# Second attention scores in two 32x64 tiles per key half, without late keys against early queries, odd heads reversed

## The chip, the cores and the metric

The program runs on one core of one Trainium2 chip. The metric is the time of one execution on the device in microseconds (us), as the median of several runs; lower is better.

## The reference

One decoder layer: a causal self attention with a latent side branch, a cross attention to a second input, and a slot mixer. The input has 64 sequences of 128 tokens of 256 values; both attentions have 16 heads of 16 values. What matters here is this, in both attentions, for every sequence and head:

```
scores = (q . k) / 4                    # 128 queries x 128 keys
scores = where(allowed, scores, NEG)    # self attention: key < query; cross attention: key <= query
attn   = softmax(scores, over keys)
out    = attn . v
```

So of each 128 x 128 square the quarter in which the keys are among the last 64 and the queries among the first 64 never counts.

## The kernel before

Everything is float32 but for the masks and the maxima (bfloat16). Three stages run one after the other, local_attention, cross_attention and slots, each over 32 pairs of sequences in a software pipeline. In each stage every engine has its own hand-written order (the functions `step`), and semaphores join them. In the cross attention the chain for the pair in work is, on TensorE (PE): first scores of sequence 0, first scores of sequence 1, second scores of sequence 0, second scores of sequence 1, values of sequence 0 and (one turn later) of sequence 1, with projections and transposes of the following pair between them.

The scores are computed twice.

- **First scores** (`scores`, L518 and L524 in the local stage, L1322 and L1328 in the cross stage): queries on the partitions. 16 small bfloat16 matmuls put the mask in (L1322), and 16 float32 matmuls with tiles of 32 rows and 64 columns add the products (L1328), 128 or 256 columns moving each. VectorE (DVE) takes the row maxima (L861, L1595) and splits each into two bfloat16 parts in `max_part`; PE turns them with one transpose through `ident_bf` (L538, L1340), and ScalarE (ACT) copies them to `max_t` (`copy_max`).
- **Second scores** (`scores_t`, L548 and L554, L1350 and L1356): keys on the partitions, as the product with the values wants them. Heads lie four to a bank, slot j of bank i; the bank index i is also the group of 32 rows of the array. 16 float32 matmuls (L1350) have a weight tile of 32 rows x 128 keys and 128 query columns moving. Then 16 bfloat16 matmuls (L1356), also of 32 rows x 128 columns, subtract the maxima through `slot_rows`. The last one lets ACT take the exponential of all four banks in one instruction (`exp`, L709, L1522).

GpSimd (POOL) zeroes what the mask forbids with four selects of four heads each (`mask_weights`, L1060, L1736); `values` (L570, L1372) waits for one select per four heads. A float32 matmul is four instructions in the trace: load, matmul, load, matmul (two passes). Each stage has 64 calls of `scores_t`.

The projections of keys (`project_k`) and values (`project_v`, L442 and L1283) are float32 matmuls with all 128 rows and columns of the array, with 256 (or 272) columns moving. In the step of ACT, `copy_max` of the previous pair stands ahead of `evac_k` of the present one.

Of the kernel before, what the change touches and what calls it, by code (L numbers as in the profile page):

```python
# [6 lines left out]
BF16 = mybir.dt.bfloat16  # L7
ALU = mybir.AluOpType
# [75 lines left out]
def decoder(nc, a, out):  # L84
    with ExitStack() as ctx:
# [12 lines left out]
        ident_bf = sb("ident_bf", [128, 128], BF16)  # L98
        with ExitStack() as kept:
            cross = CrossWeights(nc, kept, sem)  # L100
            with ExitStack() as scope:
                local_attention(nc, scope, sem, a, score_banks, side_banks, x_sb, ident, ident_bf, cross)
            slot_weights = SlotWeights(nc, kept, sem, a)
            with ExitStack() as scope:
                cross_attention(nc, scope, sem, a, score_banks, bank, x_sb, ident, ident_bf, cross, slot_weights)
            with ExitStack() as scope:
                slots(nc, scope, sem, a, out, bank, x_sb, ident, cross, slot_weights)
# [59 lines left out]
class CrossWeights:  # L167


    def __init__(self, nc, scope, sem):  # L170
# [19 lines left out]
        self.v_heads = [sb(f"v_heads{i}", [128, 2, H, HW]) for i in range(2)]  # L190
        self.max_part = sb("max_part", [128, 2, 128], BF16)
# [12 lines left out]
def local_attention(nc, scope, sem, a, score_banks, side_banks, x_sb, ident, ident_bf, cross):  # L204
# [45 lines left out]
    xn_t = sb("xn_t", [128, C, PT])  # L250
    pooled = sb("pooled", [128, C, 128])
# [49 lines left out]
    xnT_filled, xnT_ready, pooled_ready = s("xnT_filled"), s("xnT_ready"), s("pooled_ready")  # L301
    q_filled, q_ready, k_filled, k_ready = s("q_filled"), s("q_ready"), s("k_filled"), s("k_ready")
# [26 lines left out]
    with nc.Block() as block:  # L329
# [55 lines left out]
        def _(pe):  # L385
# [9 lines left out]
            def project(dst, e, first):  # L395
                for c in range(C):
                    mm = pe.matmul(dst[:, e * PT:e * PT + PT], w_qk[:, c, first + e, :], xn_t[:, c, :],  # L397
                                   start=(c == 0), stop=(c == C - 1), skip_group_check=True)
                return mm
# [33 lines left out]
            def project_v(at, tt):  # L433
                if tt == 0:
                    pe.wait_ge(k_ready, at.count(1, 1))
# [5 lines left out]
                for c in range(C):  # L441
                    mm = pe.matmul(v_bank[tt][:, 0:VW], xn_t[:, c, S * tt:S * tt + S], w_v[:, c, 0:VW],  # L442
                                   start=(c == 0), stop=(c == C - 1), skip_group_check=True)
# [53 lines left out]
            def slot(i, j):  # L497
                return score_banks[:, i, 128 * j:128 * j + 128]

            def scores(at, tt):  # L500
                if tt == 0:
                    pe.wait_ge(q_ready, at.count(1, 1))
                    pe.wait_ge(k_ready, at.count(1, 1))
                    if at.off == 0:
                        pe.wait_ge(masks_made, 14)
                        pe.wait_ge(zeroed, 13)
# [14 lines left out]
                for late in range(2):  # L521
                    for e in range(2):
                        for i in range(4):
                            mm = pe.matmul(near_far(half(e), i)[:, :, 128 * (1 - late):128 * (1 - late) + 64 * (1 + late)],  # L524
                                           q_f[at.par][group(i), e, S * tt + 64 * late:S * tt + 64 * late + 64],
                                           k_z[at.par][group(i), e, :, S * tt:S * tt + 64 * (1 + late)],
# [3 lines left out]
            def max_transpose(at, tt):  # L530
# [28 lines left out]
            def values(at, tt):  # L559
# [5 lines left out]
                for h in range(H):  # L565
                    g, j = h // 4, h % 4
                    slot_j = 2 * (j % 2) + j // 2
                    if j == 0:
                        pe.wait_ge(masked, at.count(8, 4 * tt + g + 1))
                    mm = pe.matmul(av_bank[HW * j:HW * j + HW, 128 * g:128 * g + 128], v_heads[at.par][:, tt, h, :],  # L570
                                   probs_t[tt][:, 4 * g + slot_j, :], start=True, stop=True, skip_group_check=True)
# [73 lines left out]
            pe.wait_ge(ident_made, 2)  # L645
# [4 lines left out]
        def _(act):  # L650
            def copy_xn(at):
# [3 lines left out]
                                     ACT.Copy).then_inc(xnT_ready, 1)  # L655

# [43 lines left out]
            def copy_max(at, tt):  # L700
                act.wait_ge(maxT_filled, at.count(2, tt + 1))
                wait(act, sct_filled, at.count(2, tt - 1))
                nc.scalar.activation(max_t[:, tt, :], maxT_bank[:].bitcast(BF16)[:, 0:128],
# [32 lines left out]
            def step(at):  # L736
# [8 lines left out]
                if at.real:  # L745
                    evac_k(at)
# [32 lines left out]
        def _(dve):  # L779
# [241 lines left out]
            dve.wait_ge(zeroed, 6)  # L1021
            nc.vector.memset(lat_rows[0:2, :], 0.0).then_inc(zeroed, 1)
# [6 lines left out]
            dve.wait_ge(zeroed, 13)  # L1029
# [15 lines left out]
        def _(pool):  # L1045
# [9 lines left out]
            def mask_weights(at, tt):  # L1055
                pool.wait_ge(exp_done, at.count(2, tt + 1))
                pool.sem_inc(pool_turn, 1)
                for g in range(4):
                    probs = probs_t[tt][:, 4 * g:4 * g + 4, :]
                    nc.gpsimd.affine_select(out=probs, in_=probs, pattern=[[0, 4], [1, 128]], compare_op=ALU.is_ge,  # L1060
                                            fill=0.0, base=-1, channel_multiplier=-1).then_inc(masked, 1)
# [57 lines left out]
            pool.wait_ge(ident_made, 1)  # L1119
            nc.gpsimd.tensor_copy(ident_bf[:], ident[:]).then_inc(ident_made, 1)  # L1120
# [32 lines left out]
def cross_attention(nc, scope, sem, a, score_banks, bank, x_sb, ident, ident_bf, cross, slot_weights):  # L1153
# [24 lines left out]
    ctx_t = sb("ctx_t", [128, C, PT])  # L1178
    q_f = [sb(f"q_f{i}", [128, 2, PT]) for i in range(2)]
# [22 lines left out]
    xnT_filled, xnT_ready, ctxT_filled, ctxT_ready = s("xnT_filled"), s("xnT_ready"), s("ctxT_filled"), s("ctxT_ready")  # L1202
    q_filled, q_ready, k_filled, k_ready = s("q_filled"), s("q_ready"), s("k_filled"), s("k_ready")
# [20 lines left out]
    with nc.Block() as block:  # L1224
# [17 lines left out]
        def _(pe):  # L1242
# [18 lines left out]
            def project(dst, e, first, src):  # L1261
                for c in range(C):
                    mm = pe.matmul(dst[:, e * PT:e * PT + PT], cross.w_qk[:, c, first + e, :], src[:, c, :],  # L1263
                                   start=(c == 0), stop=(c == C - 1), skip_group_check=True)
# [12 lines left out]
            def project_v(at, tt):  # L1277
                if tt == 0:
                    pe.wait_ge(k_ready, at.count(1, 1))
                else:  # L1280
                    pe.wait_ge(q_ready, at.count(1, 1))
                for c in range(C):
                    mm = pe.matmul(v_bank[tt][:, 0:D], ctx_t[:, c, S * tt:S * tt + S], cross.w_v[:, c, :],  # L1283
                                   start=(c == 0), stop=(c == C - 1), skip_group_check=True)
# [19 lines left out]

            def slot(i, j):
                return score_banks[:, i, 128 * j:128 * j + 128]

            def scores(at, tt):
# [16 lines left out]
                for late in range(2):  # L1325
                    for e in range(2):
                        for i in range(4):
                            mm = pe.matmul(near_far(half(e), i)[:, :, 128 * (1 - late):128 * (1 - late) + 64 * (1 + late)],  # L1328
                                           q_f[at.par][group(i), e, S * tt + 64 * late:S * tt + 64 * late + 64],
                                           k_z[at.par][group(i), e, :, S * tt:S * tt + 64 * (1 + late)],  # L1330
# [3 lines left out]
            def max_transpose(at, tt):  # L1334
# [5 lines left out]
                pe.transpose(maxT_bank[:].bitcast(BF16)[:, 0:128], max_part[:, tt, :], ident_bf[:]).then_inc(maxT_filled, 1)  # L1340

            def scores_t(at, tt):
# [4 lines left out]
                toks = slice(S * tt, S * tt + S)  # L1347
                for j in range(4):
                    for i in range(4):
# [905 lines left out]
```

## Time and profile before

| | us |
|---|---|
| median of three runs | 1481.04 (1479.7 to 1481.35) |
| the profiled execution | 1480.41 |
| its span in the profile | 1478.7 |
| PE busy | 1407.6 (95%) |
| DVE busy | 1088.6 (74%) |
| ACT busy | 900.5 (61%) |
| POOL busy | 823.5 (56%) |
| mean granted TensorE clock | 0.982 of full speed |

The span is counted from the first to the last instruction; 1.7 us lie around it. Engines: PE is TensorE's matmuls, PEld its weight loads, which overlap them. A busy PE is not PE at its peak, since matmuls are pipelined and overlap; what a block of them costs is read from where the next block starts. By the timeline the local stage ends near 690 us and the cross stage near 1165 us. L12 is line 12 of the kernel.

### The profile page before, as it was taken

How to read it: one execution, taken by the hardware profiler on the slowest of the kernel's cores; microseconds unless marked ns; L12 is line 12 of the kernel's file. 1: busy time of each engine (PE TensorE's matmuls, PEld its weight loads, DVE VectorE, ACT ScalarE, POOL GpSimd, SP SyncE). 2: the span in 40 equal slices, each digit the busy share in tenths (PEclk: the TensorE clock that was granted, in tenths of full speed). 3: DMA queues.
4: the chain of work that ended last, by engine and by line, in shares of the span. 5: the costliest groups of instructions: out<-in, count | busy, mean ns of one | idle time of the engine just before them, and what ended most of it. 6: DMA issues, size and time to landing. Idle time of an engine off the chain costs nothing. (4 is left out here: it accounts for less than half of the span.)

```text
span 1478.7 us, 57208 instructions
## 1 busy us (share of the span) xinstructions
PE 1407.6 (95%) x22238; PEld 1064.8 (72%) x22238; DVE 1088.6 (74%) x3025; ACT 900.5 (61%) x1573; POOL 823.5 (56%) x1152
## 2 busy tenths in 40 slices
PE   6999999999999999996999999999999949999997
PEld 4777777777777777774777777777777726766675
DVE  6777777777777777763477777777777748999996
ACT  2555555555555655553667676666667537778774
POOL 3455445554455544554377777877777753333442
PEclk9999999999999999997999999999999969999999
DMA  5500000000000000000300000000000000101111
GB/s 164 156 4 1 0 0 0 0 0 0 0 0 0 0 0 0 1 2 18 109 17 16 20 14 21 14 21 14 21 14 14 3 1 16 37 29 35 35 36 43
DMA packets 31207, 32.40 MB, mean 22 GB/s; under 512 B 3937, under 2 KB 29602, under 8 KB 31138
## 3 DMA queue, kind: packets, MB, share of 16 engines
q1 hardware_dynamic: 31138, 31.46, 6.9%
q8 instruction: 46, 0.75, 0.2%
q14 instruction: 23, 0.19, 0.0%
HBM read 23.06 MB, written 8.39 MB: 21 GB/s over the span
## 5 line engine op out<-in xcount | busy, mean ns | idle before, releaser
L1060 POOL TENSOR_SCALAR_AFFINE_SELECT a_probs_t<-a_probs_t 128x512 f32<-128x512 f32 x256 | 162.4, 669 | 62.2 <-ACT a_probs_t L709 62.2
L1595 DVE TENSOR_REDUCE c_neg_max<-score_banks 128x8 f32<-128x512 f32 (+1 forms) x128 | 116.6, 953 | 82.7 <-PE score_banks L1328 82.7
L1074 POOL TENSOR_TENSOR a_less<-a_attn,a_remote 128x512 f32<-128x512 f32 x32 | 40.8, 1274 | 218.1 <-DVE a_attn L884 218.1
L1736 POOL TENSOR_SCALAR_AFFINE_SELECT c_probs_t<-c_probs_t 128x512 f32<-128x512 f32 x256 | 153.8, 638 | 14.6 <-ACT c_probs_t L1522 13.8
L709 ACT ACTIVATE a_probs_t<-score_banks 128x2048 f32<-128x2048 f32 x64 | 120.2, 1878 | 47.0 <-PE score_banks L554 47.0
L1522 ACT ACTIVATE c_probs_t<-score_banks 128x2048 f32<-128x2048 f32 x64 | 120.3, 1879 | 26.2 <-PE score_banks L1356 26.2
L397 PE MATMUL side_banks<-a_xn_t,a_w_qk 128*128 128x256 f32 x512 | 134.7, 398 | 1.6 <-ACT a_xn_t L654 0.7
L861 DVE TENSOR_REDUCE a_neg_max<-score_banks 128x8 f32<-128x512 f32 (+1 forms) x128 | 116.4, 951 | 5.9 <-PE score_banks L524 5.9
L397 PEld LDWEIGHTS side_banks<-a_xn_t,a_w_qk 128*128 128x128 f32 x512 | 93.2, 197 | 13.0 <-issue 2.3
L2164 POOL TENSOR_TENSOR r_hn<-rz_t,half_hn 128x256 f32<-128x256 f32 x32 | 23.3, 729 | 138.5 <-ACT rz_t L1992 138.5
L664 ACT ACTIVATE a_k_z<-side_banks,a_b_k,row_half 128x256 f32<-128x256 f32 x128 | 61.8, 563 | 53.7 <-PE side_banks L397 53.7
L1529 ACT ACTIVATE c_av_t<-side_banks 128x512 f32<-128x512 f32 x64 | 39.2, 612 | 86.9 <-PE side_banks L1372 86.9
L1927 PE MATMUL side_banks<-w_ih,gi_t 128*128 128x512 f32 (+1 forms) x256 | 88.0, 486 | 0.4 <-DVE n_in L2093 0.3
L1485 ACT ACTIVATE c_k_z<-side_banks,b_k_half,row_half 128x256 f32<-128x256 f32 x128 | 61.9, 563 | 34.2 <-PE side_banks L1263 34.2
L1747 POOL TENSOR_TENSOR c_scaled<-c_normed,gamma 128x512 f32<-128x512 f32 x32 | 40.6, 1268 | 73.0 <-DVE c_normed L1577 73.0
L1350 PEld LDWEIGHTS score_banks<-c_q_f,c_k_z 32*128 32x128 f32 x2048 | 62.9, 186 | 22.6 <-ACT c_probs_t L1522 12.1
L548 PE MATMUL score_banks<-a_q_f,a_k_z 32*128 32x128 f32 x2048 | 75.1, 283 | 2.7 <-DVE a_neg_max L861 2.7
L548 PEld LDWEIGHTS score_banks<-a_q_f,a_k_z 32*128 32x128 f32 x2048 | 62.9, 186 | 19.7 <-DVE a_neg_max L861 13.0
L1350 PE MATMUL score_banks<-c_q_f,c_k_z 32*128 32x128 f32 x2048 | 75.1, 283 | 1.8 <-ACT c_probs_t L1522 1.8
L442 PE MATMUL side_banks<-a_w_v,a_xn_t 128*128 128x272 f32 x256 | 74.2, 412 | 0.0
L1927 PEld LDWEIGHTS side_banks<-w_ih,gi_t 128*128 128x128 f32 x256 | 48.4, 190 | 35.2 <-issue 31.5
L826 DVE TENSOR_TENSOR v_heads<-side_banks,a_b_v 128x272 f32<-128x272 f32 x64 | 28.0, 437 | 57.7 <-issue 49.3
(264 smaller groups left out, 3901.9 us busy)
## 6 DMA issues: line engine op xcount, KB each, us to landing
x_sb<-in_x SPq DMA_DIRECT2D x32, 256.0 KB, 3.0
ctx_in<-in_ctx SPq DMA_DIRECT2D x32, 256.0 KB, 2.7
out<-y SPq DMA_DIRECT2D x32, 256.0 KB, 2.1
w_ih<-in_ffn_w_ih SPq DMA_DIRECT2D x1, 768.0 KB, 4.8
w_hh<-in_ffn_w_hh SPq DMA_DIRECT2D x1, 768.0 KB, 6.0
a_raw_qk<-in_attn_qk_w SPq DMA_DIRECT2D x1, 512.0 KB, 3.8
a_raw_cross<-in_xattn_qk_w SPq DMA_DIRECT2D x1, 512.0 KB, 4.6
b_ih<-in_ffn_b_ih SPq DMA_DIRECT2D x1, 384.0 KB, 6.6
```

Source lines behind the costliest of these rows:

```text
L397: mm = pe.matmul(dst[:, e * PT:e * PT + PT], w_qk[:, c, first + e, :], xn_t[:, c, :], start=(c == 0), stop=(c == C - 1), skip_group_check= ...
L442: mm = pe.matmul(v_bank[tt][:, 0:VW], xn_t[:, c, S * tt:S * tt + S], w_v[:, c, 0:VW], start=(c == 0), stop=(c == C - 1), skip_group_check= ...
L548: pe.matmul(slot(i, j), k_z[at.par][group(i), j // 2, j % 2, toks], q_f[at.par][group(i), j // 2, toks], start=(j == 0), stop=False, skip_ ...
L709: nc.scalar.activation(probs_t[tt][:].rearrange("p h q -> p (h q)"), score_banks[:].rearrange("p b n -> p (b n)"), ACT.Exp, scale=SCALE).t ...
L861: ins = nc.vector.tensor_reduce(neg_max[:, tt, :].rearrange("p (i s l) -> p i s l", i=4, s=2)[:, :, :, late], all_scores[:, :, :, 128 * (1 ...
L1060: nc.gpsimd.affine_select(out=probs, in_=probs, pattern=[[0, 4], [1, 128]], compare_op=ALU.is_ge, fill=0.0, base=-1, channel_multiplier=-1 ...
L1350: pe.matmul(slot(i, j), k_z[at.par][group(i), j // 2, j % 2, toks], q_f[at.par][group(i), j // 2, toks], start=(j == 0), stop=False, skip_ ...
L1485: ins = nc.scalar.activation(k_z[at.par][:, e, half, :], k_bank[:, e * PT:e * PT + PT], ACT.Relu, bias=cross.b_k[:, half, e:e + 1], scale= ...
L1522: nc.scalar.activation(probs_t[tt][:].rearrange("p h q -> p (h q)"), score_banks[:].rearrange("p b n -> p (b n)"), ACT.Exp, scale=SCALE).t ...
L1595: ins = nc.vector.tensor_reduce(neg_max[:, tt, :].rearrange("p (i s l) -> p i s l", i=4, s=2)[:, :, :, late], all_scores[:, :, :, 128 * (1 ...
L1736: nc.gpsimd.affine_select(out=heads, in_=heads, pattern=[[0, 4], [1, 128]], compare_op=ALU.is_ge, fill=0.0, base=0, channel_multiplier=-1) ...
L1927: mm = pe.matmul(gate_bank[b][:, 0:hi - lo], gi_t[:, c, :], w.w_ih[:, c, lo:hi], start=(c == 0), stop=(c == C - 1))
```

## The change

In both attentions (not only in the cross attention) the second scores leave out the quarter of late keys and early queries. Each of the 16 matmuls of `scores_t` becomes two with weight tiles of 32 rows x 64 keys: the early keys with all 128 queries, the late keys with the 64 late queries. For odd heads (e = 1) keys and queries are taken in reverse order, so that the short product of an odd head falls into the half of the array that has the long product of the even head. The order of the heads in the banks changes to j = 2s + e. The left-out quarter is filled by the 16 maxima matmuls, which remain 32 x 128: two more rows of `max_part` are set to -1e30, and `slot_rows` has a one there for the keys concerned.

What the reversal brings with it: the key projection of odd heads reads its moving operand backwards; ACT makes a reversed copy of the transposed input (`reverse`, once per pair, between `copy_max` and `evac_k`); `project_v` takes 4 matmuls with half the columns in place of 2; the first scores, the second scores and the values read one moving operand backwards for odd heads; the transpose of the maxima becomes a bfloat16 matmul with the matrix `turned`; the selects go over every second head, and `values` waits for two selects per eight heads. Six small DVE instructions are added ahead of the first loop, one small POOL cast is removed.

The core of the diff (the cross attention; the local one has the same edits, with xn_rev for ctx_rev):

```diff
             def project(dst, e, first, src):
                 for c in range(C):
-                    mm = pe.matmul(dst[:, e * PT:e * PT + PT], cross.w_qk[:, c, first + e, :], src[:, c, :],
-                                   start=(c == 0), stop=(c == C - 1), skip_group_check=True)
+                    toks = src[:, c, :].rearrange("p (t k) -> p t k", t=2)
+                    mm = pe.matmul(dst[:, e * PT:e * PT + PT], cross.w_qk[:, c, first + e, :],
+                                   toks[:, :, ::-1] if first and e else toks, start=(c == 0), stop=(c == C - 1), skip_group_check=True)
...
             def project_v(at, tt):
                 if tt == 0:
+                    pe.wait_ge(reversed_, at.count(1, 1))
                     pe.wait_ge(k_ready, at.count(1, 1))
...
-                for c in range(C):
-                    mm = pe.matmul(v_bank[tt][:, 0:D], ctx_t[:, c, S * tt:S * tt + S], cross.w_v[:, c, :],
-                                   start=(c == 0), stop=(c == C - 1), skip_group_check=True)
+                for e in range(2):
+                    for c in range(C):
+                        toks = (ctx_rev if e else ctx_t)[:, c, S * tt:S * tt + S]
+                        mm = pe.matmul(v_bank[tt][:, 0:D].rearrange("p (h e n) -> p e h n", e=2, n=HD)[:, e],
+                                       toks,
+                                       cross.w_v[:, c, :].rearrange("p (h e n) -> p e h n", e=2, n=HD)[:, e],
+                                       start=(c == 0), stop=(c == C - 1), skip_group_check=True)
...
-                pe.transpose(maxT_bank[:].bitcast(BF16)[:, 0:128], max_part[:, tt, :], ident_bf[:]).then_inc(maxT_filled, 1)
+                pe.matmul(maxT_bank[:, 0:128], max_part[:, tt, :], cross.turned[:], start=True, stop=True,
+                          skip_group_check=True).then_inc(maxT_filled, 1)
...
-                toks = slice(S * tt, S * tt + S)
                 for j in range(4):
-                    for i in range(4):
-                        pe.matmul(slot(i, j), k_z[at.par][group(i), j // 2, j % 2, toks],
-                                  q_f[at.par][group(i), j // 2, toks], start=(j == 0), stop=False, skip_group_check=True)
+                    e = j % 2
+                    for late in range(2):
+                        rows, early, side = half(late ^ e), S * tt + 64 * late, late * (1 - e)
+                        for i in range(4):
+                            keys = k_z[at.par][group(i), e, j // 2, S * tt:S * tt + S][:, 64 * (late ^ e):64 * (late ^ e) + 64]
+                            queries = q_f[at.par][group(i), e, early:S * tt + S]
+                            pe.matmul(score_banks[rows, i, 128 * j + 64 * side:128 * j + 64 * side + 64 * (2 - late)],
+                                      keys, queries[:, ::-1] if e else queries,
+                                      start=(j == 0), stop=False, skip_group_check=True)
...
-                        by_row = score_banks[:, i, :].rearrange("p (e j r) -> p j e r", e=2, j=4)
-                        mm = pe.matmul(by_row[:, j], cross.slot_rows[group(i), j, :],
+                        quarters = score_banks[:, i, :].rearrange("p (s b r) -> p s b r", s=2, r=64)[:, j // 2]
+                        mm = pe.matmul(quarters[:, 1:3, :] if j % 2 else quarters[:, 0::3, :], cross.slot_rows[group(i), j, :],
...
-                    if j == 0:
-                        pe.wait_ge(masked, at.count(8, 4 * tt + g + 1))
+                    if h % 8 == 0:
+                        pe.wait_ge(masked, at.count(8, 4 * tt + g + 2))
...
+            def reverse(at):
+                act.wait_ge(ctxT_ready, at.count(1, 1))
+                wait(act, v_filled, at.count(2, 0))
+                nc.scalar.activation(ctx_rev[:].rearrange("p c (t k) -> p (c t) k", t=2),
+                                     ctx_t[:].rearrange("p c (t k) -> p (c t) k", t=2)[:, :, ::-1],
+                                     ACT.Copy).then_inc(reversed_, 1)
```

## Rows read from the trace of the kernel before

**Rows 1.** Page, part 1: busy time of each engine, its share, instructions.

```profile
PE 1407.6 (95%) x22238; PEld 1064.8 (72%) x22238; DVE 1088.6 (74%) x3025; ACT 900.5 (61%) x1573; POOL 823.5 (56%) x1152
```

**Rows 2.** Busy time by stretch (us, PE, PEld, DVE, ACT, POOL, clock, DMA, GB/s).

```profile
300.00:400.00 100.00, 99.26 (x1756) 75.64 (x1757) 72.86 (x182) 57.01 (x98) 54.02 (x70) 1.00 0.00 0
900.00:1000.00 100.00, 98.92 (x2014) 77.97 (x2007) 74.73 (x186) 65.90 (x111) 76.07 (x108) 1.00 0.07 18
```

**Rows 3.** Page, part 5: the score matmuls of both stages, with their counts.

```profile
L548 PE MATMUL score_banks<-a_q_f,a_k_z 32*128 32x128 f32 x2048 | 75.1, 283 | 2.7 <-DVE a_neg_max L861 2.7
L1350 PE MATMUL score_banks<-c_q_f,c_k_z 32*128 32x128 f32 x2048 | 75.1, 283 | 1.8 <-ACT c_probs_t L1522 1.8
```

**Rows 4.** Timeline, PE, cross stage, from 803 us (start us, busy us, engine, line).

```profile
803.12 1.03 PE L1263 MATMUL side_banks<-c_ctx_t,w_qk_b 128*128 128x256 f32 x4
803.99 1.03 PE L1263 MATMUL side_banks<-c_xn_t,w_qk_b 128*128 128x256 f32 x4
...
804.95 1.17 PE L1350 MATMUL score_banks<-c_q_f,c_k_z 32*128 32x128 f32 x32
...
805.94 0.40 PE L1356 MATMUL score_banks<-c_max_t,slot_rows 32*128 32x128 bf16 x16
...
806.27 1.13 PE L1263 MATMUL side_banks<-c_xn_t,w_qk_b 128*128 128x256 f32 x4
...
808.32 1.17 PE L1350 MATMUL score_banks<-c_q_f,c_k_z 32*128 32x128 f32 x32
...
810.61 0.60 PE L1292 MATMUL side_banks<-ident,c_q_f 128*128 128x128 f32 x4
...
811.05 0.60 PE L1257 MATMUL side_banks<-ident,ctx_in 128*128 128x128 f32 x4
```

**Rows 5.** Timeline, PE, local stage: the latent projections with 64 columns of the array.

```profile
301.22 0.66 PE L421 MATMUL side_banks<-a_xn_t,a_w_lat 128*64 128x128 f32 x8
...
301.70 0.40 PE L426 MATMUL side_banks<-a_pooled,a_w_lat 128*64 128x64 f32 x8
...
302.04 0.66 PE L429 MATMUL side_banks<-a_w_v,a_pooled 128*128 128x64 f32 x4
```

**Rows 6.** Timeline, PE: start of one call of the first scores.

```profile
816.68 0.32 PE L1322 MATMUL score_banks<-mask_b,mask_to_b 32*64 32x128 bf16 x16
```

**Rows 7.** That call: L1328 loads started by 816.86, 816.95, 817.00 and 817.15 us.

```profile
L1328 PEld LDWEIGHTS score_banks<-c_k_z,c_q_f x16: 128/132/133, 816.8 to 816.8; 32*64 32x64 f32 x16
L1328 PEld LDWEIGHTS score_banks<-c_k_z,c_q_f x17: 128/132/133, 816.8 to 816.9; 32*64 32x64 f32 x17
L1328 PEld LDWEIGHTS score_banks<-c_k_z,c_q_f x20: 127/132/133, 816.8 to 817.0; 32*64 32x64 f32 x20
L1328 PEld LDWEIGHTS score_banks<-c_k_z,c_q_f x32: 127/132/133, 816.8 to 817.1; 32*64 32x64 f32 x32
```

**Rows 8.** One line's instructions in one call: duration ns min/median/max, first and last start.

```profile
L1322 PE MATMUL score_banks<-mask_b,mask_to_b x16: 214/226/238, 816.7 to 816.8; 32*64 32x128 bf16 x16
L1350 PE MATMUL score_banks<-c_q_f,c_k_z x32: 270/270/372, 804.9 to 805.9; 32*128 32x128 f32 x32
```

**Rows 9.** Timeline, cross stage: ACT's work between PE blocks, and PE behind it.

```profile
804.19 1.93 ACT L1485 ACTIVATE c_k_z<-side_banks,b_k_half,row_half 128x256 f32<-128x256 f32 x4 [1.04 <-PE side_banks L1263]
...
806.38 1.88 ACT L1522 ACTIVATE c_probs_t<-score_banks 128x2048 f32<-128x2048 f32 x1 [0.26 <-PE score_banks L1356]
...
813.53 0.63 ACT L1529 ACTIVATE c_av_t<-side_banks 128x512 f32<-128x512 f32 x1
...
814.22 0.66 PE L1383 MATMUL side_banks<-ident,c_av_t 128*128 128x128 f32 x4
```

**Rows 10.** Timeline, cross stage: the selects of sequence 1 and the values that use them.

```profile
813.34 2.40 POOL L1736 TENSOR_SCALAR_AFFINE_SELECT c_probs_t<-c_probs_t 128x512 f32<-128x512 f32 x4
...
815.67 1.08 PE L1372 MATMUL side_banks<-c_probs_t,v_heads 128*32 128x128 f32 x32
```

**Rows 11.** Timeline: DVE's first wait for PE after its set-up.

```profile
17.63 0.35 DVE L814 TENSOR_SCALAR a_rq_f<-side_banks,a_b_lat 128x128 f32<-128x128 f32 x1 [2.70 <-PE side_banks L429]
```

More of the change, by code:

```diff
@@ L745, in step @@
                 if at.real:
+                    reverse(at)
                     evac_k(at)
@@ L1021, in _ @@
             dve.wait_ge(zeroed, 6)
+            for e in range(2):
+                turned = ident[:, 64 * e:64 * e + 64]
+                nc.vector.tensor_copy(cross.turned[:, 64 * e:64 * e + 64], turned[:, ::-1] if e else turned).then_inc(zeroed, 1)
+                early = cross.slot_rows[:, 0::2, 64 * (1 - e):64 * (1 - e) + 64]
+                nc.vector.tensor_scalar(early, early, cross.diagonal[:, 8 + e:9 + e], None, ALU.add).then_inc(zeroed, 1)
+                nc.vector.memset(max_part[64 * e:64 * e + 64, :, 8 + e::32], NEG).then_inc(zeroed, 1)
             nc.vector.memset(lat_rows[0:2, :], 0.0).then_inc(zeroed, 1)
@@ L1057, in mask_weights @@
                 pool.sem_inc(pool_turn, 1)
[L1058 to L1061, printed above, removed]
+                for g in range(2):
+                    for e in range(2):
+                        four, sign = probs_t[tt][:, 8 * g + e:8 * g + 8:2, :], 1 - 2 * e
+                        nc.gpsimd.affine_select(out=four, in_=four, pattern=[[0, 4], [sign, 128]], compare_op=ALU.is_ge,
+                                                fill=0.0, base=-1, channel_multiplier=-sign).then_inc(masked, 1)
             def bias_x(at):
@@ L1262, in project @@
                 for c in range(C):
-                    mm = pe.matmul(dst[:, e * PT:e * PT + PT], cross.w_qk[:, c, first + e, :], src[:, c, :],
-                                   start=(c == 0), stop=(c == C - 1), skip_group_check=True)
+                    toks = src[:, c, :].rearrange("p (t k) -> p t k", t=2)
+                    mm = pe.matmul(dst[:, e * PT:e * PT + PT], cross.w_qk[:, c, first + e, :],
+                                   toks[:, :, ::-1] if first and e else toks, start=(c == 0), stop=(c == C - 1), skip_group_check=True)
                 return mm
@@ L1278, in project_v @@
                 if tt == 0:
+                    pe.wait_ge(reversed_, at.count(1, 1))
                     pe.wait_ge(k_ready, at.count(1, 1))
@@ L1339, in max_transpose @@
                     pe.wait_ge(maxT_ready, at.count(2, 1))
-                pe.transpose(maxT_bank[:].bitcast(BF16)[:, 0:128], max_part[:, tt, :], ident_bf[:]).then_inc(maxT_filled, 1)
+                pe.matmul(maxT_bank[:, 0:128], max_part[:, tt, :], cross.turned[:], start=True, stop=True,
+                          skip_group_check=True).then_inc(maxT_filled, 1)
             def scores_t(at, tt):
@@ L1346, in scores_t @@
                     pe.wait_ge(exp_done, at.count(2, 1))
-                toks = slice(S * tt, S * tt + S)
                 for j in range(4):
-                    for i in range(4):
-                        pe.matmul(slot(i, j), k_z[at.par][group(i), j // 2, j % 2, toks],
-                                  q_f[at.par][group(i), j // 2, toks], start=(j == 0), stop=False, skip_group_check=True)
+                    e = j % 2
+                    for late in range(2):
+                        rows, early, side = half(late ^ e), S * tt + 64 * late, late * (1 - e)
+                        for i in range(4):
+                            keys = k_z[at.par][group(i), e, j // 2, S * tt:S * tt + S][:, 64 * (late ^ e):64 * (late ^ e) + 64]
+                            queries = q_f[at.par][group(i), e, early:S * tt + S]
+                            pe.matmul(score_banks[rows, i, 128 * j + 64 * side:128 * j + 64 * side + 64 * (2 - late)],
+                                      keys, queries[:, ::-1] if e else queries,
+                                      start=(j == 0), stop=False, skip_group_check=True)
                 pe.wait_ge(maxT_ready, at.count(2, tt + 1))
```

81 lines of the change are left out of this document (47 added, 34 removed).

## Prediction

> **What bounds the kernel now.** I read the page first: PE is busy 95% of the span, the next engine 74% [rows 1]. Then the busy time by stretch: in the steady part of both attention stages PE is busy for 99 of 100 us at full clock, and nobody else over 78 (the weight loads) [rows 2]. Then PE's timeline. So in both stages the time is PE's order of work, block after block, and an edit is worth what it adds to or takes from the distance between the starts of two blocks. Two prices hide between the blocks. Four passes of 256 columns take 0.87 us (803.12 to 803.99), but 0.96 us when a block with another tile shape follows (803.99 to 804.95): PE stands 0.09 us at a change of tile shape [rows 4]. And the score block of 32 instructions, 8 rounds of four tiles side by side, takes 0.99 us (804.95 to 805.94), where 8 rounds at 0.110 us (four passes of 128 columns in the 0.44 us from 810.61 to 811.05) make 0.88: the first pass after a change costs about 0.11 more [rows 4]. With loads of 64 columns that extra is smaller: 301.22 to 301.70 is 0.48 us for four rounds of 0.110, so 0.04 to 0.05 [rows 5]. A call of the second scores with the maxima takes 804.95 to 806.27 = 1.32 us, of which 0.33 us belong to the 16 maxima and the change of shape behind them. There are 2 x 2048 / 32 = 128 calls [rows 3].
>
> **The change, part by part.**
>
> (1) *The columns saved.* A half of the array gets 128, 64, 128 and 64 columns in place of four times 128, two passes each. A 64-column round is 0.06 us: 301.70 to 302.04 is 0.34 us for four rounds and a change of 0.09 [rows 5]. If both halves are always fed, the block is 2 x (0.11 + 0.06 + 0.11 + 0.06) + 0.05 = 0.73 us. That is 0.26 us less than 0.99, and 33 us over 128 calls; this is what the edit is good for at best.
>
> (2) *The instructions it takes.* The block goes from 64 instructions (loads and matmuls) to 128, all of them short. What happens beyond 64 is visible in the first scores. Their first matmul starts at 816.68 [rows 6]. 16 mask matmuls with their loads are 32 instructions, the 16 loads of L1328 started by 816.86 stand for another 32; in the next 0.09 us just one load starts, and then three in 0.05 us, 0.017 us apart, each the head of a float32 matmul of four instructions; all 32 have started by 817.15 [rows 7]. So 64 instructions stand ready, and the 65th and later come in only when the first of them are through: the first mask matmul lasts 0.214 us [rows 8], and the stream resumes some 0.05 us after that. I read it as a queue of 64 whose places come free in order. In the new block the first 64 instructions are j = 0 and j = 1. They run to 0.05 + 2 x (0.11 + 0.06) = 0.39 us. The first matmul's second pass starts at 0.16 us, lasts 0.27 us [rows 8] and is through at 0.43. The loads of j = 2 then come at 0.48, 0.50, 0.51 and 0.53 (128 columns) and up to 0.60 (64 columns), those of j = 3 from 0.61 to 0.66 and up to 0.73. With 0.05 us per load, the half that runs the short products of j = 2 is free at 0.72 to 0.77, and the long ones of j = 3 follow on it for 0.22 us: the block ends at 0.94 to 0.99. I take 0.97 us; bounds are 0.91 (places free 0.06 earlier) and 1.05 (later by as much again).
>
> (3) *A change of shape within the call.* The 32x64 block is followed by maxima in 32x128. No row shows just this pair of shapes. The bounds are nothing, since the rows of the array are cut in the same way, and 0.09 us, which every change in the rows costs, also the one from 128x64 to 128x128, where only the columns change [rows 4, 5]. I take 0.09, as that row is the nearest. The Trainium skill (TensorEngine Tiling (Array Packing), Key Properties) says that a change of tiling mode, not of the tile alone, drains the engine; the rows agree with 0.09 us each, and by it this change is paid too. The first round of the maxima also pays an extra of 0 to 0.05 us; I take 0.03.
>
> (4) *Sum per call.* 0.97 + 0.09 + 0.03 + 0.33 = 1.42 us against 1.32: 0.10 us more, 128 times, +12.8 us. It breaks even with a block of 0.87 us.
>
> (5) *project_v.* Four passes of 0.217 become eight of 0.110: +0.01 us. In the cross stage both calls lie in stretches that end on ACT anyway: the exponential ends at 806.38 + 1.88 = 808.26 and PE's next score block starts at 808.32; the copy ends at 814.16 and PE starts at 814.22 [rows 4, 9]. There it is free; without that cover it would be 0.6 us in all. In the local stage it counts: 64 x 0.01 = +0.6 us.
>
> (6) *ACT's reversed copy.* 512 elements like the copy of 0.63 us, in a place where ACT waits 1.04 us for the key projection [rows 9]. Nothing; were the gap gone, 0.6 us per pair, 20 us per stage. PE's new wait for it comes several blocks later, with the second sequence's projections queued behind it.
>
> (7) *Selects and waits.* The last eight heads wait for the fourth select, which ends at 815.74; PE reaches them at 815.67 + 0.54 = 816.21 [rows 10]. Covered by 0.47 us, nothing; the first eight have over 1 us. The selects are as large as before.
>
> (8) *Set-up.* Six small DVE instructions, well under 2 us together, ahead of a wait of 2.70 us for PE [rows 11]. Nothing. The turning of the maxima stays one bfloat16 matmul with 128 columns.
>
> (9) *Backward reads.* No row shows one. Bound below: nothing, as it is the same number of elements. Above: a pass of double length. I take nothing: every change named above leaves the count of elements alone, and the upper end is rival D.
>
> The profiled execution of 1480.4 us becomes 1480.4 + 12.8 + 0.6 = 1493.8; the median of the runs lies 0.6 us above it, so 1494.4. I say 1494 us, with 1486 to 1502 from the bounds of (2) and (3).
>
> **The rivals.**
>
> *A, faster: all eight tiles are fed.* If the places in the queue come free early enough, the block takes 0.73 us, a call 0.73 + 0.09 + 0.03 + 0.33 = 1.18, 0.14 less: 1481 - 18 + 0.6 = 1464 us. It decides as soon as the block is under 0.87 us, 0.10 below my reading. Against it stands the pause in rows 7. The Trainium skill has the rule behind it (same page and section: tiles operate independently and load and multiply in parallel), and taken alone it gives this 1464. It also gives a queue depth of 64 for TensorE (TensorE: Matmul & The Clock Gate, the section on the array as 16 sub-arrays), with which the trace agrees. Chance 0.10.
>
> *B, a little faster: places come free out of order.* Then the short passes, through by 0.3 us, make room for j = 2 before its half is idle, and the block takes about 0.80 us: 0.07 less per call, 1481 - 9 + 0.6 = 1473 us. Against it: in rows 7 loads that were long done made no room. Chance 0.12.
>
> *C, no change: no stop between 32x64 and 32x128.* The call is 0.97 + 0.33 = 1.30 us, 1481 - 2.6 + 0.6 = 1479 us. Chance 0.10.
>
> *D, much slower: backward reads at half pace.* The key projection alone has four such passes of 0.217 us a pair: 64 x 0.87 = +56 us on top, 1550 us or more. Chance 0.04.
>
> **How the numbers follow.** My case has 0.62, 0.02 is left for anything else. A measurement of this kernel tells 0.2%, 3 us, from no change. Faster by more: A, B and a little of C, 0.25. Within it: C and the lowest end of mine, 0.11. Slower: 0.64. The range 1468 to 1502 takes in B, C and mine, and leaves out A, D and mine's upper end, under 2 in 10.
>
> **What would show it.** L1350's successor: right if its block lasts 0.91 to 1.05 us from first start to the first maxima less 0.09, with a pause of its loads after the 64th instruction; wrong if the loads run through and the maxima start 0.82 us (0.73 + 0.09) after the block does. Step 3: the maxima start 0.09 us after the last pass ends. Step 5: eight passes 0.11 apart. Step 6: ACT's reversed copy is followed by a shorter wait for PE, and PE shows no wait for it. D would show in the key projection: passes of 0.43 us where e = 1. A distance of 803.99's and 806.27's successors (a whole call) over 1.32 + 0.09 us makes it slower, under 1.32 faster.

## The result and the profile after

The changed kernel takes 1522.11 us (median of 4 runs, 1520.71 to 1524.25), the kernel before 1480.37 us on the same chip (4 runs, 1479.12 to 1481.35): a ratio of 1.0283, with an interval of 1.0270 to 1.0297. It is 41.7 us slower; 13 were forecast, with an upper end of 1502. The page of the changed kernel: parts 1 to 3, then its largest group of score matmuls in each stage.

```profile
span 1522.5 us, 66385 instructions
PE 1425.3 (94%) x26846; PEld 1090.0 (72%) x26846; DVE 1089.2 (72%) x3031; ACT 933.2 (61%) x1637; POOL 821.4 (54%) x1151
...
GB/s 172 141 3 4 3 3 3 3 3 3 3 3 3 3 3 3 3 3 3 107 24 17 20 16 19 19 15 21 14 21 14 3 1 8 36 35 34 34 35 42
...
q8 instruction: 163, 2.67, 0.7%
...
L559 PE MATMUL score_banks<-a_q_f,a_k_z 32*64 32x64 f32 (+1 forms) x4096 | 71.3, 256 | 2.9 <-DVE a_neg_max L881 2.9
L1388 PE MATMUL score_banks<-c_q_f,c_k_z 32*64 32x64 f32 (+1 forms) x4096 | 70.7, 254 | 1.8 <-ACT c_probs_t L1568 1.8
```

PE's busy share hardly moved [rows 1]. What is new is the GB/s line: 3 or 4 through the whole local stage (slices 3 to 19), where no input is loaded, and a queue named "instruction" with 163 packets of 16 KB, by which the engine's program is brought in. In the kernel before it has 46. By stretch, the same two as in [rows 2]:

```profile
300.00:400.00 100.00, 92.40 (x1832) 71.12 (x1834) 66.61 (x162) 52.81 (x90) 48.88 (x64) 0.98 0.01 3
900.00:1000.00 100.00, 99.18 (x2497) 78.84 (x2495) 77.43 (x188) 69.69 (x119) 75.83 (x103) 1.00 0.06 16
```

The cross stage is as dense as before; the local stage lost 7 us in 100 and a little of its clock. The timeline of PE there, around the ends of two turns of its loop (a turn is two pairs; PE runs 13 turns, so it jumps back 12 times), shows where:

```profile
258.37 1.99 PE L609 MATMUL side_banks<-a_w_out,a_mix_t 128*128 128x256 f32 x8
...
262.52 0.44 PE L523 MATMUL score_banks<-a_mask,a_mask_to 32*64 32x128 bf16 x16 [2.16 <-issue]
262.71 1.53 PE L530 MATMUL score_banks<-a_k_z,a_q_f 32*64 32x128 f32 x32
...
303.57 1.99 PE L609 MATMUL side_banks<-a_w_out,a_mix_t 128*128 128x256 f32 x8
...
308.01 0.32 PE L523 MATMUL score_banks<-a_mask,a_mask_to 32*64 32x128 bf16 x16 [2.45 <-issue]
```

and the same place before the change:

```profile
269.57 1.99 PE L597 MATMUL side_banks<-a_w_out,a_mix_t 128*128 128x256 f32 x8
...
271.50 0.32 PE L518 MATMUL score_banks<-a_mask,a_mask_to 32*64 32x128 bf16 x16
```

The last matmuls of a turn (project_out, eight of them) and the first of the next turn (the masks of scores) stand 1.93 us apart before and 4.15 and 4.44 after. PE stands there, "issue": it waits for nothing that the profile shows. It does so 12 times, once at each return, for 1.9 to 2.5 us by the idle time of the trace (2.1 to 2.6 when counted from where the last matmul should have ended at the pace of those before it). From the start of that last matmul to the first mask are 31.3 us in all, where 12 times 0.31 were before, so 27.6 us more. Two more lines of the changed kernel, one from PE's waits over the whole span (us in total, times, longest), one from the DMA view of 250 to 296 us, one turn:

```profile
PE score_banks L523 <- issue: 26.7, 12, 2.5
```

```profile
q8 instruction: 9, 0.15, 1.4%
```

Nine packets of 16 KB are fetched in every turn. The kernel before has none from 130 to 570 us. At each of the 12 stops one packet starts 2.8 to 3.3 us before PE's first matmul of the new turn and takes 0.9 to 1.4 us. Behind five of the twelve stops the granted clock falls from 2.4 to 1.2 GHz for 3.4 us (windows behind the stop at 262 us, which drops, and that at 308, which doesn't):

```profile
262.80:266.20 3.40, 3.40 (x56) 2.39 (x40) 1.82 (x2) 0.00 (x0) 0.00 (x0) 0.54 0.03 5
...
309.00:312.40 3.40, 3.40 (x90) 2.45 (x88) 2.98 (x9) 1.22 (x2) 0.00 (x0) 1.00 0.02 5
```

A turn with such a stretch is some 1.5 us longer: another 7.7 us in five of them.

Now the part that was forecast, the call in the cross stage (PE's timeline, of the changed kernel):

```profile
813.68 1.10 PE L1388 MATMUL score_banks<-c_q_f,c_k_z 32*64 32x128 f32 x64
814.72 0.40 PE L1395 MATMUL score_banks<-c_max_t,slot_rows 32*128 32x128 bf16 x16
815.05 0.48 PE L1293 MATMUL side_banks<-c_xn_t,w_qk_b 128*128 128x256 f32 x1
```

The call takes 1.370 us (median of 124) against 1.327 before (median of 122; the one in [rows 4] is read as 1.32); the block itself streams for 0.945 us, the maxima follow 0.093 us later. 128 times 0.043 is 5.5 us. Beyond its two calls a pair takes another 0.02 us in either stage (below), 1.4 us over 64 pairs. Together 27.6 + 7.7 + 5.5 + 1.4 make 42.2 us, against 41.7 measured.

So two questions went to the chip. What are the stops, and would the change cost only some 7 us without them? And is the call understood?

### The profile page after: what moved, and what is told of

It reads as the page before. It is cut to its first block and busy times, and to the rows that moved or that the text cites. A ratio compares the mean times of both kernels' runs of the same rounds, so it can differ in the third digit from the quotient of the medians.

```text
span 1522.5 us, 66385 instructions
## 1 busy us (share of the span) xinstructions
PE 1425.3 (94%) x26846; PEld 1090.0 (72%) x26846; DVE 1089.2 (72%) x3031; ACT 933.2 (61%) x1637; POOL 821.4 (54%) x1151
## 5 line engine op out<-in xcount | busy, mean ns | idle before, releaser
L717 ACT ACTIVATE a_remote<-side_banks 128x544 f32<-128x544 f32 x32 | 19.9, 623 | 91.2 <-PE side_banks L492 91.2
L559 PE MATMUL score_banks<-a_q_f,a_k_z 32*64 32x64 f32 (+1 forms) x4096 | 71.3, 256 | 2.9 <-DVE a_neg_max L881 2.9
L1388 PE MATMUL score_banks<-c_q_f,c_k_z 32*64 32x64 f32 (+1 forms) x4096 | 70.7, 254 | 1.8 <-ACT c_probs_t L1568 1.8
L559 PEld LDWEIGHTS score_banks<-a_q_f,a_k_z 32*64 32x64 f32 x4096 | 58.1, 132 | 20.0 <-DVE a_neg_max L881 11.2
L582 PE MATMUL side_banks<-a_probs_t,v_heads 128*32 128x128 f32 x2048 | 70.6, 279 | 0.8 <-issue 0.8
```

The source lines that it names most:

```text
L559: pe.matmul(score_banks[rows, i, 128 * j + 64 * side:128 * j + 64 * side + 64 * (2 - late)], keys, queries[:, ::-1] if e else queries, sta ...
L1388: pe.matmul(score_banks[rows, i, 128 * j + 64 * side:128 * j + 64 * side + 64 * (2 - late)], keys, queries[:, ::-1] if e else queries, sta ...
```

## The experiments

Times stand beside runs of the kernel before on the same chip, 1478.6 to 1480.8 us in all groups. Runs 4 to 8 were made once each; they tell of stops and lengths in the trace, not of a few us.

**1. cross_only**: the edit in the cross attention alone, the local attention as before.

> The change in the cross attention alone, the local attention as before. Theory (long local loop): PE's local loop has 1486 instructions in the program before and 1768 after, the cross loop 1545; only the long one makes PE stop at its end, so here the local stage has no stops of 2 us and the kernel takes before + 64 calls x 0.05 = +3 us, 1484. Rival (the stops come with the new waits, the reversed copy or the smaller tiles wherever they are): stops appear in the cross stage too, +20 us or more.

1484.72 us, ratio 1.0038 [1.0023, 1.0054]; no stop, 50 instruction packets. The rival is out, and the edit costs 4.8 us in the cross stage. By the trace a pair takes 15.06 us there before and 15.17 now, of which the two calls are 0.086; over 32 pairs that is 3.5 of the 4.8.

**2. local_unrolled**: the whole change, with PE's program of the local stage written out pair by pair.

```diff
-            pairs(pe, step, TAIL, ahead=1)
+            unrolled(step, TAIL)      # for k in range(NPAIR + TAIL): step(At(0, k))
```

> The changed kernel with PE's local loop written out (32 pairs, no branch), the same matmuls in the same order. Theory (fetching at the branch): no stops of 2.3 us, no half-clock stretches behind them, 1522 - 27 - 8 and about 3 less for the loop's own overhead: 1483 to 1488. Rival (the stops come from data or semaphores of the local stage): they stay, 1520 or so. Rival (too many instructions to be fetched at all): stops everywhere, slower than 1522.

1487.42 us, ratio 1.0053 [1.0038, 1.0068]. Same matmuls, same waits, and the stops and the half-clock stretches in the local stage are gone, with 34.7 us, where 27.6 + 7.7 were read from the trace. A pair takes 20.69 us in the mean, 20.58 before. 137 packets are fetched and none of them is waited for: it isn't the fetching that costs, it is the fetching behind a jump.

**3. before_unrolled**: the kernel before with both of PE's loops written out, to see whether it pays for its jumps too.

> The kernel before with PE's local and cross loops written out, nothing else. Theory: straight code is fetched in time, no stops; what goes is 0.28 us per turn of the local loop (pairs take 20.45 and 20.73 us in turn), 12 x 0.28 = 3 us, and little in the cross stage: 1477. Rival (straight code costs fetches that show as stops): slower than 1481.

1480.52 us, ratio 1.0004 [0.9995, 1.0013], a miss: nothing is gained. Of the 0.28 us by which the second pair of a turn is longer, 0.18 stay in the written-out loop (20.45 and 20.63 us in turn), so a jump to code that is still there costs at most 0.1 us per turn. Writing loops out is no gain in itself.

**4. pad_32 and 5. pad_72**: is it the length? Every matmul as before, and the local loop made longer by increments of a semaphore that nobody waits for, 4 or 9 of them behind each matmul of four parts. The cut shows project_v; the other parts have the same two lines, and pad_72 has `range(9)`.

```diff
                     mm = pe.matmul(v_bank[tt][:, 0:VW], xn_t[:, c, S * tt:S * tt + S], w_v[:, c, 0:VW],
                                    start=(c == 0), stop=(c == C - 1), skip_group_check=True)
+                    for _ in range(4):
+                        pe.sem_inc(pads, 1)
                 mm.then_inc(v_filled, 1)
```

> The kernel before with 4 increments of a semaphore that nobody waits for behind each of TensorE's project_k, project_q, project_v and project_out parts of the local stage, so that the program of its local loop grows from 1486 to 1614 instructions; nothing that is computed changes. Theory (the stops of the changed kernel come from the length of the program between the loop's branch and its return, and 7 blocks of 256 instructions still stay in the engine): no stop over 1 us at the loop's return, the instruction queue carries about 50 packets, 1480 to 1484 us (the increments cost at most some hundredths of a microsecond each turn). Rival (the stop comes from any growth of the loop): 12 stops of 2 to 2.6 us, about 1510 us.

> The same with 9 increments at each place: 1774 instructions in the local loop, as long as the changed kernel's 1768, with every matrix multiplication that of the kernel before. Theory (length of the loop's program alone): a stop of 2.1 to 2.6 us at each of the 12 returns, 9 packets of 16 KB on the instruction queue in each turn (about 150 in all), some stretches at half clock behind them, 1508 to 1522 us. Rival (the stops belong to the 32x64 tiles or to the waits of the changed kernel, not to the length): no stop over 1 us, 1480 to 1486 us.

Whether there are stops came out as the theory said. pad_32 has none over 1 us at the return (0.8 us of idle, 0.2 where a pair ends without a jump) and 48 packets; pad_72 has one at each of the 12 returns and 158 packets. So neither the 32x64 tiles nor the new waits are needed for a stop. How long they are did not: 4.1 to 4.9 us of idle where 2.1 to 2.6 were forecast, with a second stop of 1.5 to 2.1 us behind (where a pair of pad_72 ends without a jump PE is idle for 0.4 to 1.0 us). One return of pad_72:

```profile
284.10 0.44 PE L523 MATMUL score_banks<-a_mask,a_mask_to 32*64 32x128 bf16 x16 [4.80 <-issue]
284.29 0.68 PE L529 MATMUL score_banks<-a_k_z,a_q_f 32*64 32x128 f32 x16
286.56 1.16 PE L529 MATMUL score_banks<-a_k_z,a_q_f 32*64 32x256 f32 x16 [1.58 <-issue]
```

On the times both miss by far, 1532.3 and 2041.5 us: an increment isn't nearly free (below), so these two runs tell of stops, not of times.

**6. shift_215 and 7. shift_240**: or is it the place? The changed kernel, with 215 or 240 such increments run once, ahead of the local loop, whose 1768 instructions only move.

```diff
+            for _ in range(215):
+                pe.sem_inc(pe_turn, 1)
             pairs(pe, step, TAIL, ahead=1)
```

> The changed kernel with 215 increments of a semaphore that nobody waits for in TensorE's program once ahead of the local loop; the loop keeps its 1768 instructions and starts 215 places later in memory. Theory (what counts is how many blocks of 256 instructions the loop touches: 7 stay in the engine, 8 do not; the boundary's place is known to about 30 instructions only): if the loop now starts within 24 instructions behind a boundary the stops vanish and the kernel takes about 1488 us; otherwise they stay as they were, 1520 to 1525 us. Rival (only the number of instructions counts, not their place): the stops stay, 1520 to 1525 us, for this shift and the next alike.

> The same with 240 increments. Theory (blocks touched): one of this shift and the one of 215 is the likelier to bring the loop's start just behind a boundary; there the 12 stops of 2.1 to 2.6 us vanish, the instruction queue falls from 163 packets to about 70, and the kernel takes about 1488 us. Rival (only the length counts): the stops stay and it takes 1520 to 1525 us.

1538.0 and 1558.7 us. PE's timeline of shift_215 shows what to take off, the 215 increments ahead of the first key projection:

```profile
41.22 5.18 PE L400 MATMUL side_banks<-a_xn_t,a_w_qk 128*128 128x256 f32 x12 [32.10 <-issue]
```

32.1 us of idle against 0.7 in the changed kernel, so 31.4 / 215 = 0.146 us each; 35.3 / 240 in shift_240 is 0.147. Less these, shift_240 comes to 1523 us, the changed kernel's time, and it has 12 stops as well. shift_215 comes to 1507 us and has 6 stops, at every second return:

```profile
197.25 1.99 PE L609 MATMUL side_banks<-a_w_out,a_mix_t 128*128 128x256 f32 x8
...
201.70 0.32 PE L523 MATMUL score_banks<-a_mask,a_mask_to 32*64 32x128 bf16 x16 [2.46 <-issue]
...
242.96 1.99 PE L609 MATMUL side_banks<-a_w_out,a_mix_t 128*128 128x256 f32 x8
...
244.88 0.32 PE L523 MATMUL score_banks<-a_mask,a_mask_to 32*64 32x128 bf16 x16
```

(110 packets in all.) The forecasts had allowed two outcomes for each shift, no stop at all or all 12; shift_240 is the second, shift_215 is neither. Together they contradict the rival, by which only the length counts and both shifts give the same: 25 instructions of place halve the stops of the same loop.

**8. half_block**: the changed kernel without the second scores of slots 2 and 3, so with half of the block (32 loads and 32 matmuls, which is 64 instructions). The scores of these slots are left out.

> The changed kernel with the second scores of slots j = 2 and 3 left out (their probabilities come from the maxima alone); 16 matmuls, 64 instructions a call. Theory (a queue of 64 places freed in order): the score block lasts 0.05 + 2 x 0.17 = 0.39 us, so the other half of the columns costs 0.945 - 0.39 = 0.55 us in the changed kernel. Rival (small tiles are slow as such, each at 1.4 times its columns): the block is half of 0.945, 0.47 us. The local loop is 256 instructions shorter, 1512: by the loop theory no stops.

PE's timeline of this kernel:

```profile
901.62 0.59 PE L1388 MATMUL score_banks<-c_q_f,c_k_z 32*64 32x128 f32 x32
902.14 0.40 PE L1395 MATMUL score_banks<-c_max_t,slot_rows 32*128 32x128 bf16 x16
```

The half streams for 0.431 us (0.52 less the 0.093 of the change of shape), the second half of the full block for 0.945 - 0.431 = 0.514. By columns the second should be the shorter, as it has no change of shape ahead. The 0.431 lies halfway between the theory's 0.39 and the rival's 0.47, so by itself it decides nothing; what speaks for the theory is that the second half is 0.08 longer than the first, and the starts of the loads: the first 32 start at the same distances in both kernels (all within 0.29 us), and the gap comes only behind them (below). This kernel (1433.2 us) has no stops either; its local loop has 1512 instructions.

**9. cross_only_max64** and **10. unrolled_max64**: the change of shape inside the call taken out, by maxima in 32x64 tiles too: 32 instructions in place of 16. In 9 on top of cross_only, in 10 on top of local_unrolled, in both stages.

```diff
-                        quarters = score_banks[:, i, :].rearrange("p (s b r) -> p s b r", s=2, r=64)[:, j // 2]
-                        mm = pe.matmul(quarters[:, 1:3, :] if j % 2 else quarters[:, 0::3, :], cross.slot_rows[group(i), j, :],
+                        for w in range(2):
+                            quarters = score_banks[half(w), i, :].rearrange("p (s b r) -> p s b r", s=2, r=64)[:, j // 2]
+                            mm = pe.matmul(quarters[:, 1:3, :] if j % 2 else quarters[:, 0::3, :],
+                                           cross.slot_rows[group(i), j, half(w)],
```

> The change in the cross attention alone, with the first 16 maxima matrix multiplications of each call split into 32 of 32x64 tiles, so that the call never changes its shape of tile after its first instruction. cross_only took 1484.7 us, with 1.37 us per call (score block 0.945, change of shape 0.093, maxima 0.241, and 0.09 around them). Theory (TensorE waits for the array to drain where the shape changes, and that is the 0.093): the gap between the two blocks falls to 0.03 or less, the maxima block stays at 0.24 to 0.30 since its 32 instructions of half the load are fed at 16.6 ns each at best and come to 0.53 us if the feeding sets it; a call takes 1.29 to 1.35 us and the kernel 1480 to 1484 us. Rival (32 small instructions are bound by their feeding, not by columns): the maxima block grows to 0.45 to 0.55 us, a call takes over 1.5 us, and the kernel 1493 us or more. A second rival: the cross loop's program, 1673 instructions long, brings stops at its return, 12 of 2.3 us, whatever the call does.

> The whole change with TensorE's local loop written out (local_unrolled, 1487.4 us) and the maxima in 32x64 tiles in both stages. Theory: both stages gain what cross_only_max64 gains over cross_only, twice, so 1479 to 1485 us; this is the only form of the change that could reach the kernel before. Rival (feeding of the 32 small instructions): 1505 us or more.

1595.26 us, ratio 1.0766 [1.0744, 1.0789], and 1599.99 us, ratio 1.0810 [1.0783, 1.0837]. Theory and feeding rival of both texts miss these times; the second rival of the first text decides both: the cross loop, now of 1673 instructions, stops at every return. From PE's timeline of cross_only_max64, one return:

```profile
908.78 0.44 PE L1338 MATMUL score_banks<-mask_b,mask_to_b 32*64 32x128 bf16 x16 [4.87 <-issue]
```

The stops are 3.8 to 5.0 us here, more than in the changed kernel's local stage, with a second one of 1.7 to 2.4 us some 3 us on, and 7 to 10 us of half clock behind each: 110 us in 12 turns. Why they are twice as long was not settled. That the 32x64 maxima themselves change nothing shows beside it: a call lasts 1.365 us (median of 64) against 1.369 in cross_only. The maxima now start 0.82 us into the call instead of 1.04, before the scores have ended, but from there to the next block it is 0.545 us where it was 0.332 with 16 instructions.

**11. cross_max64_unrolled**: run 9 with PE's cross loop written out.

> cross_only_max64 with TensorE's cross loop written out turn by turn, so that it has no return and no stop at one. Theory 1 (the extra 110 us of cross_only_max64 all come from its loop of 1673 instructions and none from the 32x64 maxima, whose call takes 1.365 us in the trace against 1.370 of cross_only): 1481 to 1486 us, the time of cross_only. Theory 2 (the small maxima instructions cost time of their own, by their feeding): over 1490 us. Either way the change of shape inside a call would be worth less than 0.3 us in all, against the 11.5 us that the prediction's step 3 gave it.

1484.68 us, ratio 1.0038 [1.0024, 1.0052], against cross_only's 1484.72. The 110 us were all the loop's, within the 2 us that the intervals leave.

**What the places say.** In the compiled programs PE's loops lie as follows (places of their first and last instruction, 64 bytes each, so that a 16 KB packet holds 256):

```
kernel, loop                first   last  count  stops
before, local                2186   3671   1486  none
half_block, local            2254   3765   1512  none
cross_only, cross            8172   9716   1545  none
changed, cross               9324  10868   1545  none
pad_32, local                2410   4023   1614  none
cross_only_max64, cross      8364  10036   1673  every return
changed, local               2638   4405   1768  every return
shift_240, local             2878   4645   1768  every return
pad_72, local                2690   4463   1774  every return
shift_215, local             2853   4620   1768  every second return
```

The packet counts fit the lengths. The whole program of PE is 11920 instructions before (46 packets, as the queue shows) and 14224 after, 55 packets, and 55 + 12 x 9 is the 163 of the queue. pad_72's program is as long as that of cross_only, which took 50, and 50 + 12 x 9 is its 158; shift_215's fills 56, and 56 + 6 x 9 is its 110. So each stop goes with nine packets that are fetched again, and a loop without stops is fetched once.

If packets begin at places of 13 to 37 beyond a multiple of 256, the first five loops touch seven packets and the four that stop at every return touch eight; shift_215 touches seven and ends within 24 places of its seventh's end. Seven packets would then stay in the engine and eight not. That nine are fetched per turn fits one fetched ahead: the eight of the loop and one behind it, which takes a place that the next turn needs. The place of the boundary is fitted to these runs, and the fetching ahead is argued, not measured. The same fit would put the starts of the loops with stops of 1.9 to 2.5 us at most 65 places behind a boundary, and those of pad_72 and cross_only_max64, with 3.8 to 5.0 us, at least 93; whether that is what makes a stop long, no run tests. The Trainium skill (Runtime: NRT & Kernel Launch, Instruction fetch mechanics) gives PE 2048 instructions of memory, as a FIFO refilled in blocks of 256, and says that a taken branch to code that isn't there waits for its fetch; eight blocks is 2048, and the trace agrees with that, but not with the two-page window that the same section names, since seven stayed.

## Why the prediction was wrong

The direction was right, and so was the block. The size was not, because a term was missing; that 1522 lies on the forecast's side of 1481 says nothing for the sum, as 35 of the 41.7 us come from what it didn't hold.

*What failed: the list of what could cost, steps 1 to 9.* Step 2 counted the block's instructions, 64 to 128, for PE's queue and for nothing else. The same growth lengthens PE's local loop from 1486 to 1768 instructions (four calls in a turn with 64 more each, 32 of project_v, six waits fewer), and no step asked what the loop's jump costs: the forecast put it at nothing without a reason. Run 2 shows that it is 35 of the 42 us in this kernel, run 11 that it is 110 in another. The profile of before gave a hint, the instruction queue with its 46 packets and a steady stage without one; where the limit lies it did not tell.

*(1), (2) The block.* 0.94 to 0.99 us was forecast, 0.97 taken, 0.945 measured; A (0.73) and B (0.80) are out. The pause behind the 64th instruction is there. Loads of one call of L1388 started by 813.9, 814.0, 814.1, 814.2 and 814.45 us (the block starts at 813.7):

```profile
L1388 PEld LDWEIGHTS score_banks<-c_q_f,c_k_z x28: 127/131/133, 813.7 to 813.9; 32*64 32x64 f32 x28
L1388 PEld LDWEIGHTS score_banks<-c_q_f,c_k_z x32: 127/132/133, 813.7 to 814.0; 32*64 32x64 f32 x32
L1388 PEld LDWEIGHTS score_banks<-c_q_f,c_k_z x34: 127/132/133, 813.7 to 814.1; 32*64 32x64 f32 x34
L1388 PEld LDWEIGHTS score_banks<-c_q_f,c_k_z x39: 127/131/133, 813.7 to 814.2; 32*64 32x64 f32 x39
L1388 PEld LDWEIGHTS score_banks<-c_q_f,c_k_z x64: 127/131/133, 813.7 to 814.4; 32*64 32x64 f32 x64
```

28 loads in the first 0.2 us, 11 in the next 0.3, 25 in the last 0.25. By the starts in the trace the 32nd load comes 0.29 us into the block, the next three at 0.33, 0.39 and 0.46, and the other 29 from 0.475 to 0.765. Step 2 had the 33rd at 0.48, when both passes of the first matmul are through; it comes 0.15 us earlier, some 0.06 behind the end of the first pass (0.27). That the 0.025 us between 0.97 and 0.945 are these early loads is likely, not shown. half_block, with its 64 instructions, shows 0.431 with no pause.

*(3) The change of shape* costs 0.093 us, as taken; the extra of 0.03 for the maxima's first round isn't there (from the first maxima to the next block it is 0.332 us before and after). But the 0.093 isn't there to be had either: run 9 removes it and a call is 0.004 us shorter. That the 32 instructions more pay it back in feeding is how I read the longer maxima block; it was not tested apart.

*(4) The sum* was +0.10 us per call and +12.8; it is +0.043 and +5.5. The two terms that were too high are the 0.97 (by 0.025) and the 0.03. Rival C (1479 us) had no stop at the change of shape and is out; the 1487 us without the loop's stops lie between it and my 1494.

*(5)* project_v's eight passes stand 0.112 us apart in the cross stage, and the call takes 0.891 us where it took 0.863: +0.03, not +0.01 (in the local stage +0.00 for the first call of a pair and +0.04 for the second); of both only 0.02 us are left in a pair's time. *(6)* ACT's reversed copy (0.62 us at 811.76) is followed by a wait of 0.55 us for PE where there were 1.04 [rows 9], and cross_only bounds all of it: project_v, ACT, selects and set-up (5 to 8) together with the calls cost 4.8 us, of which 64 calls are 2.8. *(9)* backward reads cost nothing: key projections of 0.864 us per four passes (0.216 each) before and after the reversal, so D is out.

## What to carry to other kernels

Count the instructions of an engine's loop before an edit multiplies them, and look at the instruction queue's packets in the steady part of a loop: none means that the loop stays in the engine, a constant trickle of 16 KB packets in a loop means that each return may cost 2 to 5 us, here and there with half the clock behind it. Here loops of up to 1614 instructions stayed and those of 1673 and more did not, but for one of 1768 that stayed at every second return; a loop near that size is to be shortened or written out, which cost nothing in three kernels. And halving the columns of short instructions saves little once more of them follow each other than the queue holds: with a quarter of the columns gone the block went from 0.995 us to 0.945, and the change of shape behind it took that back.

## What was not expected of the hardware

- An increment of a semaphore by PE as an instruction of its own costs 0.146 us (215 and 240 of them in a row, 31.4 and 35.3 us). In pad_32 some 2048 of them (64 per pair) cost 54 us in all, 0.026 each, so most ran beside the matmuls. The 563 us of pad_72 hold its stops and its many stretches at half clock too (mean granted clock 0.887), and what the increments alone cost there was not taken apart.
- The stop at a loop's return was 1.9 to 2.5 us in the changed kernel's local loop, 4.1 to 4.9 in the local loop of pad_72 and 3.8 to 5.0 in the cross loop of cross_only_max64, so it isn't the stage that sets it.
- The clock fell to 1.2 GHz behind 5 of 12 like stops in the changed kernel, 2 of 12 in shift_240 and 3 of 6 in shift_215; nothing that was looked at tells them apart.
- The page hides these stretches: its line of granted clock shows 9 in each of the first 19 slices, the local stage of the changed kernel.
